# A graph attention kernel whose first layer recomputes each tile's own rows on the chip instead of loading them from its table

## The chip, the cores and the metric

The kernel runs on one core of a Trainium2 chip. The metric is the device time of one execution in microseconds (us). TensorE does the matrix products, VectorE and ScalarE the element-wise work, GpSimd issues the gathers, and SyncE issues the plain loads and stores. In the rows they are PE, DVE, ACT, POOL and SP; SPq is SyncE's queue of transfers.

## The reference

`x` is 8192 x 128, `adj` is 8192 x 8192 of int32 with about nine ones in a row, the diagonal among them. Two layers follow one another:

```
h = relu(layernorm(x))
# layer 0
wh = h @ W;  s1 = wh @ a[:128];  s2 = wh @ a[128:]
e = leaky_relu(s1[i] + s2[j], 0.2) where adj[i, j] > 0, else -9e15
x = x + elu(softmax(e) @ wh)
h = relu(layernorm(x))
# layer 1
q = h @ Wq.T + bq;  k = h @ Wk.T + bk;  v = h @ Wv.T + bv
x = x + elu(softmax(q @ k.T / sqrt(128) where adj > 0) @ v)
```

## The kernel before

A row of `adj` is nearly empty, so the kernel never forms the 8192 x 8192 scores. It reads `adj` once, finds each row's neighbours, and gathers their rows from a table in HBM. The nodes are cut into 64 tiles of 128 rows, one row to a partition.

**Setup.** Every row of `x` is measured on VectorE (`rstd`, `shift`), normalised on ScalarE, turned and projected on TensorE, two tiles a step. The result, 132 words a node (`wh`, then `s2`, `s1` and a one), goes to `table0` in HBM. `s1` also stays on the chip in `self_s1`.

**Survey**, which makes layer 0. It is a pipeline written out by hand: an iteration `t` does a different step for several tiles, and every engine runs its own list in order. For tile `t + 1` ScalarE turns four quarters of 1 MB of `adj` (`read_quarter`, L1166) to a mask, and TensorE packs the mask in 16 matmuls (`pack`, L1368). VectorE extracts tile `t`'s neighbours (`extract`, L698) and lists them. For tile `t - 3` (`PICK`) it marks (L790) and picks the indices (L820), TensorE deals (L1429), and GpSimd issues nine gathers of 128 rows into `Gt[:, t % 4, 1:]` (L571). For tile `u = t - 6` (`LATE`) VectorE makes the scores (`score0`, L836), TensorE scatters them (L1401), and VectorE takes the maxima (`maxima`, L845 to L849). For tile `w = t - 7` (`DONE`) VectorE weighs (L859), adds seven rows (`add_slot`, L869 and L866), each between two extractions, TensorE sums the rest (`sum_up`, L1415), and VectorE adds both (`total`, L875) and finishes the tile. Slot 0 of `Gt` holds the tile's own row, since every node is its own neighbour: SyncE loads it from `table0` (`load_self`, L460) tile `t - 4` in iteration `t`, 66 KB a tile, in the same queue as the loads of `adj`.

SyncE issues the next quarter of `adj` when ScalarE has read the one whose place it takes (L447). Two tiles, eight quarters, can be under way. Each pair of tiles has its list decoded in the odd iteration, which makes that one longer on VectorE; the odd iteration starts with `split` (L783), which waits for a matmul at the end of TensorE's even iteration (L1453).

**Layer 1** starts when all of the survey is done. Its rows are gathered from `table1` (L601), and its own rows are loaded there too (L521).

Of the kernel before, what the change touches and what calls it, by code (L numbers as in the profile page):

```python
# [5 lines left out]
P = 128  # L6
# [6 lines left out]
ALU = mybir.AluOpType  # L13
# [17 lines left out]
OWN = 1 + REGULAR  # L31
# [10 lines left out]
def two_layer_graph_attention(nc, x, adj, W, a, Wq, bq, Wk, bk, Wv, bv, out):  # L42
# [22 lines left out]
    with ExitStack() as ctx:  # L65
# [44 lines left out]
        neg_diag = place([T])  # L110
        self_s1 = place([T, 2])
        sum_all = place([T, QUARTERS])
        count_all = place([T])
# [13 lines left out]
        owned_list = place([GROUP, CHUNKS, DEALT])  # L127
        owned = owned_list[:, :, :, 0:P]
        early = top[0]
        Gt = place([GROUP, ROWS, WIDTH])  # L130
        weighted = place([CHUNKS, P])
        acc_sb = place([2, WIDTH])
        l10 = place([2, ROWS])
# [3 lines left out]
        gap = place([2, CHUNKS])  # L137
        p10 = place([2, ROWS])
        rinv = place([2, 1])
# [18 lines left out]
        sd = place([T])  # L158
        rstd = place([T])
        shift = place([T])  # L160
        h_rows = place([2, 2, D])
# [87 lines left out]
        ends_ps = bank(7)[:, 0:2]  # L249
        bad_ps = bank(7)[0:1, 104:105]  # L250

# [59 lines left out]
        rows_in = [sem(f"rows_in{k}") for k in range(GROUP)]  # L311
        self_in = [sem(f"self_in{k}") for k in range(GROUP)]
        e_done = sem("e_done")
        score_done = sem("score_done")
# [86 lines left out]

        PICK, LATE, DONE = 3, 6, 7
        PAIRS = T // 2
        UNITS = T // 2
# [37 lines left out]
        def _(sp):  # L442
# [15 lines left out]

            def load_self(v, k):
                sp.dma_start(Gt[:, k, 0, :], table0[bass.ds(v * P + 1, P), :]).then_inc(self_in[k], 16)  # L460

            def load_group(g):
                for b in range(GROUP):
                    s = g * GROUP + b
                    if live(s, -2):
                        for q in range(QUARTERS):

                            sp.wait_ge(mask_done, QUARTERS * s + q + 1)
                            load_adj(s + 2, b % 2, q)
                    if isinstance(s, int) and s == 5:  # L470
                        sp.wait_ge(zeros_in, 32)
                        for k in range(4):
                            sp.wait_ge(table0_in[k], 16 * UNITS // 4)
                        load_self(0, 0)
                    if not isinstance(s, int) or 5 <= s < T + 4:

                        at_least(sp, summed, s - 7)
                        load_self(s - 4, b)
                    if b == 2 and (not isinstance(g, int) or 0 <= g - 3 < G):
                        sp.wait_ge(stage_done, (g - 2) * GROUP)  # L480
                        sp.dma_start(table1[1:N + 1, :].rearrange("(t p) d -> p t d", p=P)
                                     [:, bass.ds((g - 3) * GROUP, GROUP), :], stage[:, :, :]).then_inc(table1_in, 16)
# [124 lines left out]
        def _(dve):  # L607
# [225 lines left out]
            def score0(u, k, r, n):  # L833
                dve.wait_ge(rows_in[r], 16 * (ROWS - 1) * n)
                dve.wait_ge(self_in[r], 16 * n)
                nc.vector.tensor_scalar(e10[:, 0:OWN], Gt[:, r, 0:OWN, D], self_s1[:, u, 1:2], None, ALU.add).then_inc(e_done, 1)  # L836
                nc.vector.tensor_tensor(e10[:, OWN:ROWS], Gt[:, r, OWN:ROWS, D], owned_list[:, r, :, DEALT - 1], ALU.add)\
                  .then_inc(e_done, 1)
                dve.wait_ge(e_done, 2 * u + 2)
                nc.vector.scalar_tensor_tensor(out=l10[:, k, :], in0=e10[:, :], scalar=ALPHA, in1=e10[:, :],  # L840
                                               op0=ALU.mult, op1=ALU.max).then_inc(score_done, 1)
                spread_scores(u, k, r)
# [19 lines left out]
            def add_slot(tt, k, r, c, width):  # L862

                if c:
                    dve.wait_ge(chained, OWN * tt + c)
                    nc.vector.scalar_tensor_tensor(out=acc_sb[:, k, 0:width], in0=Gt[:, r, c, 0:width], scalar=p10[:, k, c:c + 1],  # L866
                                                   in1=acc_sb[:, k, 0:width], op0=ALU.mult, op1=ALU.add).then_inc(chained, 1)
                else:
                    nc.vector.tensor_scalar(acc_sb[:, k, 0:width], Gt[:, r, 0, 0:width], p10[:, k, 0:1], None, ALU.mult)\  # L869
                      .then_inc(chained, 1)  # L870

            def total(tt, k, width):
# [55 lines left out]
            def survey(g):  # L928
                for b in range(GROUP):
# [14 lines left out]
                    for n in range(PARTS):  # L944
                        if n < OWN and live(t, DONE):
                            add_slot(w, w % 2, w % GROUP, n, D + 3)
                        if live(t, 0):
                            extract(t, b, n)
                    if live(t, LATE):
                        maxima(u, u % 2)  # L950
# [135 lines left out]
            with dve.Else():  # L1086
# [20 lines left out]
                def score1(u, b, k, n):  # L1107
                    dve.wait_ge(rows_in[b], 16 * (ROWS - 1) * n)
                    dve.wait_ge(self_in[b], 16 * n)
                    dve.wait_ge(own_done, u + 1)  # L1110
# [12 lines left out]
                def attend(g):  # L1123
                    for b in range(GROUP):
# [13 lines left out]
                        if live(t, 2):  # L1138
                            dve.wait_ge(e_done, 2 * T + t - 1)
                            maxima(T + t - 2, k)  # L1140
# [16 lines left out]
        def _(act):  # L1157
# [44 lines left out]
            def survey(g):  # L1202
                for b in range(GROUP):
# [24 lines left out]
                    if live(t, DONE):  # L1228
                        post(w, w % 2, acc_sb[:, w % 2, 0:D])
                    quarter(3)  # L1230
                    if t < 3:
# [114 lines left out]
        def _(pe):  # L1346
# [72 lines left out]
            def survey(g):  # L1419
                for b in range(GROUP):  # L1420
# [11 lines left out]
                    if live(t, DONE):  # L1432
                        at_least(pe, summed, w - 1)
                        sum_up(w, w % 2, w % GROUP, D + 3)
                    if live(t, -1):

                        at_least(pe, top_done, t)
                        pack(t + 1, (b + 1) % 2, range(0, 8))
# [5 lines left out]
                    if t < 3:  # L1444
                        for i in range(12 * t, min(12 * t + 12, UNITS)):
                            turn_rows(i)
                            if i:
                                project_rows(i - 1)
                        if t == 2:
                            project_rows(UNITS - 1)  # L1450
                    if b % 2 == 0 and live(t, 2):
                        pe.wait_ge(count_done, 4 * (t // 2))
                        nc.tensor.matmul(ends_ps, upto[:, :], over16[:, :], start=True, stop=True).then_inc(ends_done, 1)  # L1453
                    if t == T + 4:
                        pe.wait_ge(bad_done, 9)
                        nc.tensor.matmul(bank(7)[:, 104:105], ones[:, 0:P], bad_row[:, :], start=True, stop=True)\
                          .then_inc(bad_summed, 1)
# [58 lines left out]
            with pe.Else():  # L1516

                def attend(g):
                    for b in range(GROUP):
# [17 lines left out]
                        if live(t, 0):  # L1537
                            pe.wait_ge(self_in[b], 16 * (G + g + 1))
                            at_least(pe, u_kept, t)
# [36 lines left out]
```

## Time and profile before

| | us |
|---|---|
| median of 3 runs | 1697.23 (1695.82 to 1697.98) |
| the profiled execution | 1699.37 |
| its span | 1697.6 |
| VectorE, GpSimd, TensorE busy in the span | 1201.7, 1137.3, 1189.3 |

The page cuts the span in 40 slices of 42.4 us. The DMA engines are busy for nine tenths in all of the first twenty, and two tenths or so from there on: the survey ends near 860 us, and layer 1 begins near 950 us. A busy time is not a bound by itself. What ends last in each stage is told by the chain and by the waits.

### The profile page before, as it was taken

The numbers are of one execution on the slowest core, as the hardware profiler recorded it, in microseconds if no ns is written. First come the engines' busy times: TensorE is split into PE (matmuls) and PEld (weight loads), VectorE is DVE, ScalarE is ACT, GpSimd is POOL, SyncE is SP. The second block draws the span as 40 slices with busy tenths as digits, with TensorE's granted clock in tenths as the row PEclk, the third lists the DMA queues.
The fourth block names the chain that finished last, engine by engine and source line by source line (L and its number), as shares of the span: only waits on it lengthen the run. The fifth ranks groups of instructions, "written<-read, shape, count | busy, mean of one in ns | idle before, by whom it ended". The sixth has DMA issues, their size and how long they took to land.

```text
span 1697.6 us, 23065 instructions
## 1 busy us (share of the span) xinstructions
PE 1189.3 (70%) x5362; PEld 930.2 (55%) x5362; DVE 1201.7 (71%) x6497; ACT 904.9 (53%) x1827; POOL 1137.3 (67%) x1206
## 2 busy tenths in 40 slices
PE   2667777777777777777765467776777677676665
PEld 1344545545545554544455466766666566666664
DVE  3567988888888888888887366656655665566655
ACT  2769877877878778887852222333233323332322
POOL 1227777766766666666666477777777777777773
PEclk9778777777777777777765555556665666666755
DMA  9869999999999999999942122222222222222221
GB/s 292 345 225 391 397 398 399 400 401 396 390 386 394 365 371 390 382 394 371 386 125 61 51 59 57 65 64 66 64 66 64 66 64 64 66 64 64 66 66 39
DMA packets 122263, 372.41 MB, mean 219 GB/s; under 512 B 34577, under 2 KB 67858, under 8 KB 89362
## 3 DMA queue, kind: packets, MB, share of 16 engines
q1 hardware_dynamic: 75458, 289.83, 44.3%
q0 software_dynamic: 38464, 81.08, 17.1%
q10 hardware_dynamic: 8208, 0.03, 0.3%
q8 instruction: 46, 0.75, 0.2%
q14 instruction: 87, 0.71, 0.1%
HBM read 358.12 MB, written 12.72 MB: 218 GB/s over the span
## 4 chain that ended last, share of the span: by engine, by line
DMA 40%; POOL 33%; issue 13%; ACT 5%; DVE 4%; PE 3%; SPq 2%; POOLq 0%; ACTq 0%; DVEq 0%
DMA arena<-in_adj_dram 37%; POOL arena L601 32%; ACT arena L1166 4%; DMA table<-arena 1%; POOL arena L571 1%; SPq L444 1%; DMA arena<-table 1%; DVE arena L658 1%; SPq L447 1%; PE psum L1368 0%; DVE arena L866 0%; PE psum L1429 0%; DMA arena<-table,arena 0%; PE psum L1393 0%; PE psum L1415 0%
## 5 line engine op out<-in xcount | busy, mean ns | idle before, releaser
L571 POOL DMA_INDIRECT arena<-table,arena x576 | 558.7, 970 | 252.5 <-issue 164.6
L601 POOL DMA_INDIRECT arena<-table,arena x576 | 550.3, 955 | 184.0 <-issue 174.9
L1166 ACT ACTIVATE arena<-arena 128x2048 bf16<-128x2048 int32 x256 | 487.9, 1906 | 163.3 <-DMA arena<-in_adj_dram 160.7
L1368 PE MATMUL psum<-arena 128*128 128x512 bf16 x1024 | 301.6, 437 | 71.7 <-ACT arena L1166 71.3
L866 DVE SCALAR_TENSOR_TENSOR arena<-arena 128x131 f32<-128x131 f32 (+1 forms) x768 | 267.3, 348 | 15.2
L1415 PE MATMUL psum<-arena 128*128 128x131 f32 (+1 forms) x768 | 200.7, 433 | 104.1 <-ACT arena L1303 102.4
L1401 PE MATMUL psum<-arena 128*128 128x18 f32 x768 | 144.6, 321 | 143.7 <-DVE arena L830 143.2
L1415 PEld LDWEIGHTS psum<-arena 128*128 128x128 f32 x768 | 179.9, 330 | 107.7 <-issue 107.7
L1368 PEld LDWEIGHTS psum<-arena 128*128 128x128 bf16 x1024 | 111.3, 118 | 221.2 <-ACT arena L1166 90.7
L1401 PEld LDWEIGHTS psum<-arena 128*128 128x128 f32 x768 | 138.5, 265 | 161.9 <-DVE arena L830 161.8
L1112 DVE CUSTOM_DVE_ANT_0 arena<-arena,psum 128x129 f32<-128x129 f32 x192 | 45.2, 286 | 226.4 <-DMA arena<-table,arena 226.4
L1408 PE MATMUL psum<-arena 128*128 128x1 f32 x768 | 137.1, 294 | 94.0 <-DVE arena L849 93.9
L1408 PEld LDWEIGHTS psum<-arena 128*128 128x128 f32 x768 | 138.1, 257 | 117.2 <-DVE arena L849 108.4
L1196 ACT ACTIVATE arena<-arena 128x7 f32<-128x7 f32 x128 | 37.9, 296 | 231.8 <-DVE arena L849 231.8
L1324 ACT ACTIVATE arena<-psum 128x384 f32<-128x384 f32 x64 | 31.5, 492 | 236.4 <-PE psum L1535 236.4
L1429 PE MATMUL psum<-arena 128*128 128x155 f32 x384 | 117.7, 476 | 27.3 <-DVE arena L790 26.9
L1534 PE MATMUL psum<-arena 128*128 128x128 f32 x384 | 119.0, 412 | 1.0 <-DVE arena L1104 1.0
L1535 PE MATMUL psum<-arena 128*128 128x129 f32 x384 | 116.7, 404 | 0.0
L1429 PEld LDWEIGHTS psum<-arena 128*128 128x128 f32 x384 | 94.8, 317 | 31.9 <-DVE arena L790 31.4
L1534 PEld LDWEIGHTS psum<-arena 128*128 128x128 f32 x384 | 103.7, 329 | 1.5 <-issue 1.5
L698 DVE MAX8 arena<-psum 128x8 f32<-128x64 f32 x512 | 104.4, 221 | 0.0
L1118 DVE CUSTOM_DVE_ANT_0 arena<-arena 128x129 f32<-128x129 f32 x448 | 101.1, 290 | 0.0
(197 smaller groups left out, 1951.7 us busy)
## 6 DMA issues: line engine op xcount, KB each, us to landing
arena<-in_adj_dram SPq DMA_DIRECT2D x256, 1024.0 KB, 22.4
arena<-table,arena POOLq DMA_INDIRECT x1152
table<-arena POOLq DMA_DIRECT2D x32, 132.0 KB, 4.5
arena<-table SPq DMA_DIRECT2D x64, 66.0 KB, 17.5
table<-arena SPq DMA_DIRECT2D x16, 256.0 KB
arena<-table SPq DMA_DIRECT2D x64, 64.0 KB, 1.9
out_dram<-arena SPq DMA_DIRECT2D x16, 256.0 KB, 2.4
arena<-in_x_dram SPq DMA_DIRECT2D x4, 0.5 KB, 12.1
```

Source lines behind the costliest of these rows:

```text
L571: pool.indirect_dma_start(Gt[:, v % GROUP, c + 1, :], None, table0, bass.IndirectOffsetOnAxis(idx_now[:, v % GROUP, c:c + 1], 0))\
L601: pool.indirect_dma_start(Gt[:, t % GROUP, c + 1, 0:D], None, table1, bass.IndirectOffsetOnAxis(idx_now[:, t % GROUP, c:c + 1], 0))\
L698: ins = nc.vector.max(words[:, b // 2, b % 2, 8 * n:8 * n + 8], V[b % 2][:, PLACE * n:PLACE * (n + 1)])
L866: nc.vector.scalar_tensor_tensor(out=acc_sb[:, k, 0:width], in0=Gt[:, r, c, 0:width], scalar=p10[:, k, c:c + 1], in1=acc_sb[:, k, 0:width] ...
L1166: nc.scalar.activation(mask[:, k, q * QUARTER:(q + 1) * QUARTER], adj_sb[:, k, q, :], ACT.Relu, accum_out=sum_all[:, bass.ds(tile, 1), q:q ...
L1368: nc.tensor.matmul(V[k], shifted[:, s, :], mask[:, k, s * 512:(s + 1) * 512], start=(s == 0), stop=False)
L1401: last = nc.tensor.matmul(by_slot_ps[k], owned[:, r, c, :], slot_e[:, k, c, :], start=(c == 0), stop=(c == CHUNKS - 1))
L1408: last = nc.tensor.matmul(max_ps[k][:, c:c + 1], mine[:, r, c * P:(c + 1) * P], neg_max[:, k, :], start=True, stop=True)
L1415: last = nc.tensor.matmul(acc_ps[k][:, 0:width], weighted[:, c, :], Gt[:, r, OWN + c, 0:width], start=(c == 0), stop=(c == CHUNKS - 1))
L1429: last = nc.tensor.matmul(deal_ps[v % 2][:, c, :], mine[:, v % GROUP, c * P:(c + 1) * P], dealt[:, v % GROUP, :], start=True, stop=True)
L1534: nc.tensor.matmul(own_ps[m][:, c, :], mine_c, ident[:, :], start=True, stop=True)
L1535: last = nc.tensor.matmul(uq_ps[m][:, c, :], mine_c, u_row[:, j, P:], start=True, stop=True)
```

## The change

In layer 0 the tile's own row is no longer loaded. ScalarE normalises the tile's 128 rows again from `X` in iteration `t = o + 4` (`NORM`), into slot 0 of `Gt`. In iteration `o + 5` (`TURN`) TensorE transposes them to PSUM, VectorE copies them to `self_hT`, and TensorE multiplies by `ww`, which gives `wh`, `s2` and `s1` of the tile in PSUM (`self_ps`, two places in bank 7). `score0` reads the own row's `s2` there in an instruction of its own, and `add_self` takes the place of the first `add_slot`. SyncE's 64 loads of the first table are gone. `rstd` and `shift` move to a place that is kept, and the accumulator is laid so that its last column is the own row's probability, which the load's column of ones gave before. The second layer still loads its own rows; only the counts of its waits differ. A matmul for the check at the end of the survey moves to bank 2.

```diff
-        acc_sb = place([2, WIDTH])
+        sums_p = place([2, D + 2 + ROWS])
+        acc_sb = sums_p[:, :, 0:D + 3]
+        p10 = sums_p[:, :, D + 2:]
...
+        self_ps = [bank(7)[:, 4 + (D + 2) * k:4 + (D + 2) * (k + 1)] for k in range(2)]
+        self_turned_ps = bank(7)[:, 384:384 + P]
...
+        NORM, TURN = 4, 5
...
-            def load_self(v, k):
-                sp.dma_start(Gt[:, k, 0, :], table0[bass.ds(v * P + 1, P), :]).then_inc(self_in[k], 16)
...
-                    if isinstance(s, int) and s == 5:
-                        sp.wait_ge(zeros_in, 32)
-                        for k in range(4):
-                            sp.wait_ge(table0_in[k], 16 * UNITS // 4)
-                        load_self(0, 0)
-                    if not isinstance(s, int) or 5 <= s < T + 4:
-
-                        at_least(sp, summed, s - 7)
-                        load_self(s - 4, b)
...
             def score0(u, k, r, n):
                 dve.wait_ge(rows_in[r], 16 * (ROWS - 1) * n)
-                dve.wait_ge(self_in[r], 16 * n)
-                nc.vector.tensor_scalar(e10[:, 0:OWN], Gt[:, r, 0:OWN, D], self_s1[:, u, 1:2], None, ALU.add).then_inc(e_done, 1)
+                dve.wait_ge(self_done, u + 1)
+                nc.vector.tensor_scalar(e10[:, 0:1], self_ps[k][:, D:D + 1], self_s1[:, u, 1:2], None, ALU.add).then_inc(e_done, 1)
+                nc.vector.tensor_scalar(e10[:, 1:OWN], Gt[:, r, 1:OWN, D], self_s1[:, u, 1:2], None, ALU.add).then_inc(e_done, 1)
...
+            def add_self(tt, k):
+                nc.vector.tensor_scalar(acc_sb[:, k, 0:D + 2], self_ps[k], p10[:, k, 0:1], None, ALU.mult).then_inc(chained, 1)
+
+            def keep_self_turned(o):
+                dve.wait_ge(self_turned, o + 1)
+                nc.vector.tensor_copy(self_hT[:, :], self_turned_ps).then_inc(self_hT_done, 1)
...
                     for n in range(PARTS):
-                        if n < OWN and live(t, DONE):
+                        if n == 0 and live(t, DONE):
+                            add_self(w, w % 2)
+                        elif n < OWN and live(t, DONE):
                             add_slot(w, w % 2, w % GROUP, n, D + 3)
                         if live(t, 0):
                             extract(t, b, n)
+                    if live(t, TURN):
+                        keep_self_turned(t - TURN)
                     if live(t, LATE):
                         maxima(u, u % 2)
...
                     if live(t, DONE):
                         post(w, w % 2, acc_sb[:, w % 2, 0:D])
+                    if live(t, NORM):
+                        o = t - NORM
+                        at_least(act, self_turned, o - GROUP + 1)
+                        nc.scalar.activation(Gt[:, o % GROUP, 0, 0:D], X[:, o, :], ACT.Relu, bias=shift[:, o:o + 1],
+                                             scale=rstd[:, o:o + 1]).then_inc(self_h_done, 1)
                     quarter(3)
...
                         sum_up(w, w % 2, w % GROUP, D + 3)
+                    if live(t, TURN):
+                        o = t - TURN
+                        pe.wait_ge(self_h_done, o + 1)
+                        at_least(pe, chained, OWN * (o - 2) + 1)
+                        nc.tensor.transpose(self_turned_ps, Gt[:, o % GROUP, 0, 0:D], ident[:, :]).then_inc(self_turned, 1)
...
+                    if live(t, TURN):
+                        o = t - TURN
+                        pe.wait_ge(self_hT_done, o + 1)
+                        nc.tensor.matmul(self_ps[o % 2], self_hT[:, :], ww[:, :], start=True, stop=True).then_inc(self_done, 1)
                     if b % 2 == 0 and live(t, 2):
                         pe.wait_ge(count_done, 4 * (t // 2))
                         nc.tensor.matmul(ends_ps, upto[:, :], over16[:, :], start=True, stop=True).then_inc(ends_done, 1)
```

TensorE before, one even iteration of the survey: scatter, deal, sum, eight packs, the maxima's spread (L1408), eight packs, the end of the pack, and the matmul that `split` waits for.

```order
L1401 MATMUL psum<-arena 128x18 x3
L1429 MATMUL psum<-arena 128x155 x3
L1415 MATMUL psum<-arena 128x131 x3
L1368 MATMUL psum<-arena 128x512 x8
L1408 MATMUL psum<-arena 128x1 x3
L1368 MATMUL psum<-arena 128x512 x8
L1374 MATMUL psum<-arena 128x128
L1375 MATMUL psum<-arena 128x512
L1453 MATMUL psum<-arena 128x2
```

TensorE now, the same iteration (L1415, L1443, L1429, L1382 and L1422 are the lines of scatter, deal, sum, pack and spread in the changed file).

```order
L1415 MATMUL psum<-arena 128x18 x3
L1443 MATMUL psum<-arena 128x155 x3
L1429 MATMUL psum<-arena 128x131 x3
L1453 MATMUL psum<-arena 128x128
L1382 MATMUL psum<-arena 128x512 x8
L1422 MATMUL psum<-arena 128x1 x3
L1382 MATMUL psum<-arena 128x512 x8
L1388 MATMUL psum<-arena 128x128
L1389 MATMUL psum<-arena 128x512
L1473 MATMUL psum<-arena 128x130
L1476 MATMUL psum<-arena 128x2
```

The transpose (L1453) stands behind the sum and ahead of the first pack, the projection (L1473) behind the last.

VectorE before, from the last extraction of an iteration to the sum of tile `w`.

```order
L866 SCALAR_TENSOR_TENSOR arena<-arena 128x131
L698 MAX arena<-psum 128x8 x2
L845 TENSOR_TENSOR arena<-arena 128x7
L847 TENSOR_TENSOR arena<-psum,arena 128x18
L849 TENSOR_REDUCE arena<-arena 128x1
L875 TENSOR_TENSOR arena<-psum,arena 128x131
```

VectorE now, the same place (L875 is the new copy, L843 to L847 are the maxima and L880 is `total` in the changed file).

```order
L864 SCALAR_TENSOR_TENSOR arena<-arena 128x131
L695 MAX arena<-psum 128x8 x2
L875 COPY arena<-psum 128x128
L843 TENSOR_TENSOR arena<-arena 128x7
L845 TENSOR_TENSOR arena<-psum,arena 128x18
L847 TENSOR_REDUCE arena<-arena 128x1
L880 TENSOR_TENSOR arena<-psum,arena 128x131
```

The copy, which waits for TensorE's transpose of the same iteration, stands ahead of the maxima and of `total`.

## Rows read from the trace of the kernel before

**Rows 1.** the chain that ended last, by engine (page, part 4; shares of the span).

```profile
DMA 40%; POOL 33%; issue 13%; ACT 5%; DVE 4%; PE 3%; SPq 2%; POOLq 0%; ACTq 0%; DVEq 0%
```

**Rows 2.** busy time of the engines in both stages; us, then busy us (count) each.

```profile
148.00:857.00 709.00, 538.36 (x2368) 360.20 (x2368) 607.13 (x3209) 564.23 (x851) 491.35 (x507) 0.77 1.01 389
950.00:1672.00 722.00, 514.38 (x2387) 469.99 (x2387) 432.47 (x2499) 214.04 (x743) 547.33 (x573) 0.61 0.25 64
```

**Rows 3.** DMA queues and issues in the survey, 148 to 857 us.

```profile
GB/s 400 396 398 396 399 396 399 397 400 403 397 401 402 398 390 398 403 376 385 404 372 393 398 333 387 399 351 380 399 373 396 374 374 402 384 346 400 379 387 382
...
q1 hardware_dynamic: 46574, 240.58, 86.2%
...
arena<-in_adj_dram SPq DMA_DIRECT2D x219, 1024.0 KB, 22.8
...
arena<-table SPq DMA_DIRECT2D x56, 66.0 KB, 17.6
```

**Rows 4.** DMA queue q1 in the second layer, 1100 to 1500 us.

```profile
q1 hardware_dynamic: 9792, 4.66, 4.0%
```

**Rows 5.** waits of VectorE, 148 to 857 us: total us, times, longest.

```profile
DVE arena L859 <- ACT arena L1200: 29.2, 36, 1.8
DVE arena L783 <- PE psum L1453: 24.1, 21, 2.1
DVE arena L875 <- PE psum L1415: 5.6, 14, 0.6
```

**Rows 6.** waits of ScalarE in the same stretch.

```profile
ACT arena L1166 <- DMA arena<-in_adj_dram: 133.5, 145, 2.8
```

**Rows 7.** six tiles in order of time: start us, us, engine, line.

```profile
172.25 0.14 DVE L845 TENSOR_TENSOR arena<-arena 128x7 f32<-128x7 f32 x1
...
173.05 3.15 PE L1368 MATMUL psum<-arena 128*128 128x512 bf16 x8
...
182.56 1.89 PE L1368 MATMUL psum<-arena 128*128 128x512 bf16 x8
...
183.70 0.15 DVE L845 TENSOR_TENSOR arena<-arena 128x7 f32<-128x7 f32 x1
...
195.45 0.14 DVE L845 TENSOR_TENSOR arena<-arena 128x7 f32<-128x7 f32 x1
...
196.16 1.89 PE L1368 MATMUL psum<-arena 128*128 128x512 bf16 x8
...
207.48 0.14 DVE L845 TENSOR_TENSOR arena<-arena 128x7 f32<-128x7 f32 x1
...
208.08 2.70 PE L1368 MATMUL psum<-arena 128*128 128x512 bf16 x8
...
220.75 0.15 DVE L845 TENSOR_TENSOR arena<-arena 128x7 f32<-128x7 f32 x1
...
221.54 2.79 PE L1368 MATMUL psum<-arena 128*128 128x512 bf16 x8
...
231.24 3.06 PE L1368 MATMUL psum<-arena 128*128 128x512 bf16 x8
...
232.00 0.14 DVE L845 TENSOR_TENSOR arena<-arena 128x7 f32<-128x7 f32 x1
```

**Rows 8.** costliest groups, 50 to 130 us: count | busy us, mean ns.

```profile
L1393 PE MATMUL psum<-arena 128*128 128x130 f32 x128 | 26.1, 337 | 10.3 <-DVE arena L685 10.3
...
L1174 ACT ACTIVATE arena<-arena 128x128 f32<-128x128 f32 x64 | 26.1, 482 | 9.9 <-PE psum L1385 9.9
...
L1385 PE MATMUL psum<-arena 128*128 128x128 f32 x64 | 14.1, 309 | 0.0
...
L685 DVE COPY arena<-psum 128x256 f32<-128x256 f32 x32 | 13.3, 417 | 14.8 <-PE psum L1385 14.8
```

**Rows 9.** VectorE at the first tile's scores.

```profile
147.03 0.23 DVE L836 TENSOR_SCALAR arena<-arena 128x7 f32<-128x7 f32 x1 [2.00 <-DMA arena<-table]
```

**Rows 10.** the same view as rows 8, 80 to 860 us.

```profile
L869 DVE TENSOR_SCALAR arena<-arena 128x131 f32<-128x131 f32 x55 | 15.5, 282 | 0.0
```

More of the change, by code:

```diff
@@ L111, in two_layer_graph_attention @@
         self_s1 = place([T, 2])
+        rstd = place([T])
+        shift = place([T])
         sum_all = place([T, QUARTERS])
@@ L128, in two_layer_graph_attention @@
         owned = owned_list[:, :, :, 0:P]
+        self_hT = place([P])
         early = top[0]
@@ L137, in two_layer_graph_attention @@
         gap = place([2, CHUNKS])
-        p10 = place([2, ROWS])
         rinv = place([2, 1])
@@ L158, in two_layer_graph_attention @@
         sd = place([T])
-        rstd = place([T])
-        shift = place([T])
         h_rows = place([2, 2, D])
@@ L249, in two_layer_graph_attention @@
         ends_ps = bank(7)[:, 0:2]
-        bad_ps = bank(7)[0:1, 104:105]
+        bad_ps = bank(2)[0:1, 480:481]
+        self_ps = [bank(7)[:, 4 + (D + 2) * k:4 + (D + 2) * (k + 1)] for k in range(2)]
+        self_turned_ps = bank(7)[:, 384:384 + P]
         own_ps = [bank(k)[:, 0:CHUNKS * P].rearrange("p (c q) -> p c q", c=CHUNKS) for k in range(2)]
@@ L312, in two_layer_graph_attention @@
         self_in = [sem(f"self_in{k}") for k in range(GROUP)]
+        self_h_done = sem("self_h_done")
+        self_turned = sem("self_turned")
+        self_hT_done = sem("self_hT_done")
+        self_done = sem("self_done")
         e_done = sem("e_done")
@@ L834, in score0 @@
                 dve.wait_ge(rows_in[r], 16 * (ROWS - 1) * n)
-                dve.wait_ge(self_in[r], 16 * n)
-                nc.vector.tensor_scalar(e10[:, 0:OWN], Gt[:, r, 0:OWN, D], self_s1[:, u, 1:2], None, ALU.add).then_inc(e_done, 1)
+                dve.wait_ge(self_done, u + 1)
+                nc.vector.tensor_scalar(e10[:, 0:1], self_ps[k][:, D:D + 1], self_s1[:, u, 1:2], None, ALU.add).then_inc(e_done, 1)
+                nc.vector.tensor_scalar(e10[:, 1:OWN], Gt[:, r, 1:OWN, D], self_s1[:, u, 1:2], None, ALU.add).then_inc(e_done, 1)
                 nc.vector.tensor_tensor(e10[:, OWN:ROWS], Gt[:, r, OWN:ROWS, D], owned_list[:, r, :, DEALT - 1], ALU.add)\
                   .then_inc(e_done, 1)
-                dve.wait_ge(e_done, 2 * u + 2)
+                dve.wait_ge(e_done, 3 * u + 3)
                 nc.vector.scalar_tensor_tensor(out=l10[:, k, :], in0=e10[:, :], scalar=ALPHA, in1=e10[:, :],
@@ L1108, in score1 @@
                     dve.wait_ge(rows_in[b], 16 * (ROWS - 1) * n)
-                    dve.wait_ge(self_in[b], 16 * n)
+                    dve.wait_ge(self_in[b], 16 * (n - G))
                     dve.wait_ge(own_done, u + 1)
@@ L1138, in attend @@
                         if live(t, 2):
-                            dve.wait_ge(e_done, 2 * T + t - 1)
+                            dve.wait_ge(e_done, 3 * T + t - 1)
                             maxima(T + t - 2, k)
@@ L1455, in survey @@
                         pe.wait_ge(bad_done, 9)
-                        nc.tensor.matmul(bank(7)[:, 104:105], ones[:, 0:P], bad_row[:, :], start=True, stop=True)\
+                        pe.wait_ge(owned_done, T)
+                        nc.tensor.matmul(bank(2)[:, 480:481], ones[:, 0:P], bad_row[:, :], start=True, stop=True)\
                           .then_inc(bad_summed, 1)
@@ L1537, in attend @@
                         if live(t, 0):
-                            pe.wait_ge(self_in[b], 16 * (G + g + 1))
+                            pe.wait_ge(self_in[b], 16 * (g + 1))
                             at_least(pe, u_kept, t)
```

## Prediction

> **What bounds the kernel now.** I read the chain of waits first: the DMA engines hold 40% of it and GpSimd 33% [rows 1]. The stages part the two. In the survey, from 148 us (the first tile's scores) to 857 us (the last quarter of `adj`), the DMA engines are busy all the time (share 1.01, 389 GB/s); in layer 1 they are a quarter busy, and GpSimd, issuing gathers, works for 547 of 722 us with its own issue gaps between [rows 2]. The change touches nothing in layer 1 but counts of waits, so I leave it at its time. Everything is decided in the survey.
>
> How long is a tile there? Queue q1 moved 240.58 MB [rows 3]. Off that go 56 own-row loads of 67.6 KB (3.79 MB) and the stores of `table1`, 12 of 262 KB or 3.15 MB by the code; 233.6 MB of `adj` at 4.194 MB a tile are 55.7 tiles. 709 us over 55.7 is 12.73 us a tile.
>
> Then I ask how near the next engine is. ScalarE waits for `adj` 133.5 us in that stretch [rows 6], 2.4 us a tile: it has room. VectorE is busy 607 of 709 us [rows 2], and its waits are small: 29.2 us for ScalarE's L1200, 24.1 us for the matmul behind the even pack, 5.6 us for the sum [rows 5], 58.9 us together. ScalarE reaches L1200 behind a quarter of `adj`, and the pack waits for the mask, so the first two are mostly DMA time seen from VectorE. Without any wait VectorE needs (709 - 59) / 55.7 = 11.67 us a tile. It stands 1.06 us a tile behind the DMA, and that is all the room that the new work has.
>
> **What the change removes.** (a) The loads: 3.79 of the 275.6 MB that went at 389 GB/s over 709 us [rows 2], 9.7 us. By packets instead: layer 1's q1 used 4.0% of 16 engines for 400 us on 9792 packets of some 500 bytes, 26 ns each [rows 4]; 56 x 128 of them on 16 engines are 11.7 us. I take 10.5 us, 0.19 a tile: the DMA's tile falls to 12.54 us. (b) The first tile's scores waited 2.00 us for the own-row load after the gathers [rows 9]; that wait goes, 2 us at most, and the gathers may be just behind it. (c) SyncE's issue of the loads: it waits for ScalarE anyway, so nothing.
>
> **What it adds.** ScalarE: one 128x128 activation a tile, 0.48 us by the row for that form [rows 8]. It stands ahead of quarter 3, but ScalarE has 2.4 us a tile of waiting: nothing, and 0.4 us a tile (22 us) if that cover were gone. TensorE: a projection of 0.34 us and a transpose of 0.31 us [rows 8], ahead of which the pack waits for masks anyway; nothing by itself.
>
> VectorE: the score of the own row, one instruction of one element. It overlaps its neighbours; I take 0.10 us, between 0 and the 0.23 us of the seven-element one [rows 9]. `add_self` replaces an instruction of 0.28 us [rows 10] by one that is an element shorter, same price, with 0 to 0.07 us more. The copy of 128 columns from PSUM: the 256-column one took 0.417 us [rows 8]; half is 0.21, which I take, the whole is the upper end.
>
> The new wait is the term that matters. The copy waits for the transpose, which TensorE issues behind `sum_up` of the same iteration, where the first pack starts now; the maxima and `total` are queued behind it on VectorE, then everything to the end of the iteration, and TensorE's spread and ScalarE's probabilities wait for the maxima. Before, VectorE went on to L845 whatever TensorE did. In six tiles one after another L845 starts at 172.25, 183.70, 195.45, 207.48, 220.75 and 232.00, and the first pack at 173.05, 182.56, 196.16, 208.08, 221.54 and 231.24 [rows 7]. The transpose would be issued at that start and end 0.31 us later, so the stall is (pack - L845 + 0.31) where positive: 1.11, 0, 1.02, 0.91, 1.10 and 0. The zeros are the iterations in which TensorE ran its sum fast. With copy and score (0.31) the mean added is 4.14 / 6 + 0.31 = 1.00 us a tile. These tiles have hardly a wait for ScalarE in them, as VectorE would run where it is the bound, so they are the right ones to take. `total` waited for the sum before, which the 5.6 us above already took out. Bounds: 0.31 if TensorE is always early, 1.11 + 0.52 = 1.6 if it is always late and the copy dear.
>
> **Page and row.** The Trainium skill (VectorE: DVE Perf Modes, Why PSUM operands drop a tier) says that an fp32 operand in PSUM holds VectorE to one element a cycle, where a single source in SBUF may go at two. For `add_self` that speaks against the change; I estimate from the page's 0.96 GHz 130 / 0.96 GHz / 2 = 0.07 us a tile, and by it the sum would be 4 us longer. No row here shows the two sources side by side; the 131-column one from SBUF took 0.28 us [rows 10], so the difference stays outside the sum.
>
> **The sum.** VectorE's tile becomes 11.67 + 1.00 = 12.67 us, against 12.54 of the DMA. The survey goes at the larger one: 12.67 - 12.73 = -0.06 us, over 55.7 tiles -3.3 us; the first wait gives -2. Further, the even iteration now ends on TensorE 0.34 us later, which `split` may see: between 0 and 28 x 0.34 = 9.5 us, I take 2, since that wait is mostly for the mask. The drain behind 857 us is gather-bound and keeps its length. Together about -3 us: the profiled execution would go from 1699.4 to 1696.4. It stands 2.1 us above the median of the runs, so I predict 1694 us for the median.
>
> **Rivals.**
> 1. The DMA stays the bound and the whole saving shows. VectorE's added work is below 0.87 us a tile if TensorE stays fast in the odd iterations and in some even ones, because its gaps get shorter. For it: the two zeros above. Against it: four of six are late. Then -10.5 - 2 = -12.5, 1685 us.
> 2. Slower: the serial chain VectorE to TensorE to VectorE. The mark releases the deal, then sum, transpose, copy, maxima, all inside one iteration, and each new iteration starts on the end of TensorE's last (`self_done`, which every `score0` waits for). If the waits for ScalarE and for `split` stay partly, because those are in the chain too, they do not pay for the stall. It decides from 1.06 us a tile on. With half of the 53.3 us of the first two waits staying, the sum is -3 + 27 = +24; with a quarter +10. I take +15 as its centre: 1712 us. For it: 12.54 beside 12.67 leaves no slack for jitter between the engines. Against it: up to eight quarters of `adj` can be stored ahead.
> 3. The change frees bytes but the survey does not go faster, as the rate of the DMA varies (333 to 404 GB/s in slices [rows 3]) for reasons outside the queue: only the first 2 us, 1695 us.
>
> **Chances.** Forecast (the two bounds meet) 0.48, its own range 1688 to 1702; rival 1 0.20; rival 2 0.27; rival 3 0.05. For the whole range I take 1684, which holds most of rival 1, to 1713, half of rival 2. A change under 0.2%, 3.4 us, can't be told from none here. Faster, below 1693.8: 0.23 of the forecast's 0.48, and 0.20 of rival 1, 0.43. Slower, above 1700.6: 0.05 of the forecast and 0.25 of rival 2, 0.30. The same: 0.27.
>
> **What would show it.** The saving: 64 fewer loads, and q1 3.8 MB lighter in the survey. The bound: ScalarE's waits for `adj` fall far below 133.5 us, the DMA share below 1.0, and VectorE's waits for ScalarE and at `split` nearly go. The stall: a new VectorE wait for the transpose of 0.5 to 0.9 us a tile, 30 to 50 us in all; under 20 us is rival 1, and with it a share of 1.01 as before. For rival 2 that wait stands beside 20 us or more of the old ones, and the last quarter of `adj` lands after 857 us. I am wrong altogether if layer 1 (950 to 1672 us) changes its length, or if the drain between does.

## The result, and the profile after

| | before, us | after, us |
|---|---|---|
| median of 20 runs | 1695.80 (1694.05 to 1699.98) | 1700.66 (1698.25 to 1703.53) |
| the profiled execution | 1699.37 | 1698.98 |
| its span | 1697.6 | 1697.2 |

The changed kernel is slower, by 4.9 us between the medians; the ratio of the paired runs is 1.0024 (95% interval 1.0017 to 1.0030), which is 4.1 us. The two profiled executions differ by 0.4 us only, the changed kernel's being the shorter. That of before was one of its slower ones, 3.6 us above its median, and that of after lies 1.7 us below its own. The traces tell where time is spent, then, but the sum is read from the runs.

The chain of the changed kernel by engine (the page, part 4), against [rows 1]:

```profile
POOL 33%; DVE 27%; PE 20%; issue 13%; ACT 4%; DMA 2%; SPq 1%; POOLq 0%; ACTq 0%; DVEq 0%
```

GpSimd's third is layer 1, as before. The DMA engines' 40% have become 2%, and VectorE and TensorE, which held 7% together, hold 47%. So the survey is bound by another thing. The engines in the two stages, the windows and columns of [rows 2]:

```profile
148.00:857.00 709.00, 551.27 (x2486) 381.08 (x2529) 621.13 (x3314) 585.93 (x911) 485.59 (x505) 0.77 1.00 382
950.00:1672.00 722.00, 503.26 (x2387) 460.20 (x2387) 433.50 (x2500) 214.87 (x744) 546.13 (x574) 0.63 0.25 64
```

Layer 1 has the same load on every engine. From its first gather to its last it takes 724.5 us before and 723.4 after; the twelve traces of this document have 723.1 to 725.2, so 1.1 us is no more than they differ by anyway. In the survey VectorE works 621 us instead of 607. The DMA share is still 1.00, although nobody waits for it, as the next rows show. The queue in that stretch, against [rows 3]:

```profile
q1 hardware_dynamic: 38338, 236.13, 84.5%
...
arena<-in_adj_dram SPq DMA_DIRECT2D x218, 1024.0 KB, 12.2
```

8236 packets are gone, most of them the own rows. A quarter of `adj` now lands 12.2 us after its issue, where it took 22.8. At 382 and 389 GB/s I estimate from this that some 4 quarters are on their way, where there were some 8: the queue is no longer full. The waits of VectorE and ScalarE, 148 to 857 us, against [rows 5, 6]:

```profile
DVE arena L875 <- PE psum L1453: 43.7, 50, 1.4
DVE arena L780 <- PE psum L1476: 6.3, 14, 0.9
```

```profile
ACT arena L1205 <- DVE arena L847: 69.5, 54, 1.7
ACT arena L1209 <- DVE arena L851: 30.5, 27, 1.8
ACT arena L1234 <- PE psum L1443: 9.1, 13, 0.8
ACT arena L1187 <- DVE arena L783: 8.1, 15, 0.7
```

VectorE waits 43.7 us for the transpose (L1453), in 50 of the 56 tiles. In this stretch ScalarE's 133.5 us of waits for `adj` are gone altogether, and it waits for VectorE's maxima instead. One even iteration shows how (start, duration, engine, line; L1429 is the sum, L875 the copy, L843 the maxima):

```profile
274.58 1.52 PE L1429 MATMUL psum<-arena 128*128 128x131 f32 x6
...
274.89 0.35 DVE L695 MAX8 arena<-psum 128x8 f32<-128x64 f32 x2
...
275.89 0.40 PE L1453 MATMUL psum<-arena 128*128 128x128 f32 x1
...
276.33 0.29 DVE L875 COPY arena<-psum 128x128 f32<-128x128 f32 x1 [1.08 <-PE psum L1453]
276.53 0.16 DVE L843 TENSOR_TENSOR arena<-arena 128x7 f32<-128x7 f32 x1
```

VectorE ends its extractions at 275.24 and stands still until the transpose is through at 276.29. The odd iteration ahead of it has the same wait, a third as long:

```profile
261.50 0.42 PE L1453 MATMUL psum<-arena 128*128 128x128 f32 x1
...
261.96 0.29 DVE L875 COPY arena<-psum 128x128 f32<-128x128 f32 x1 [0.36 <-PE psum L1453]
```

Where the time goes is read from one instruction that every iteration has, the deal. Its rows for the 1st, 5th, 11th, 57th and 61st tile that have a scatter ahead of it, first of before, then of after:

```profile
148.86 1.90 PE L1429 MATMUL psum<-arena 128*128 128x155 f32 x6
...
193.24 1.90 PE L1429 MATMUL psum<-arena 128*128 128x155 f32 x6
...
269.02 1.92 PE L1429 MATMUL psum<-arena 128*128 128x155 f32 x6 [0.66 <-DVE arena L790]
...
862.09 1.92 PE L1429 MATMUL psum<-arena 128*128 128x155 f32 x6 [1.12 <-DVE arena L790]
...
905.49 1.90 PE L1429 MATMUL psum<-arena 128*128 128x155 f32 x6
```

```profile
146.32 1.80 PE L1443 MATMUL psum<-arena 128*128 128x155 f32 x6
...
194.80 1.92 PE L1443 MATMUL psum<-arena 128*128 128x155 f32 x6
...
272.89 1.90 PE L1443 MATMUL psum<-arena 128*128 128x155 f32 x6
...
861.35 1.90 PE L1443 MATMUL psum<-arena 128*128 128x155 f32 x6
...
907.80 1.90 PE L1443 MATMUL psum<-arena 128*128 128x155 f32 x6
```

| us a tile | before | after |
|---|---|---|
| first 4 | 11.10 | 12.12 |
| next 6 | 12.63 | 13.02 |
| next 46 | 12.89 | 12.79 |
| last 4 | 10.85 | 11.61 |

The survey before had two bounds in turn. What ScalarE waited for `adj`, from 148 to 200 us and then from 200 to 269 us:

```profile
ACT arena L1166 <- DMA arena<-in_adj_dram: 0.5, 1, 0.5
...
ACT arena L1166 <- DMA arena<-in_adj_dram: 13.1, 15, 2.8
```

In the first four tiles ScalarE hardly waited for `adj`, so the DMA did not bound them, and the new work on VectorE and its wait cost 4.1 us there. From 200 us on the DMA was the bound. The next six tiles lose another 2.3 us, and the 46 behind them win 4.6 us.

The last four deals come 3.1 us further apart in all, but what counts there is when the gathers end and layer 1 can start. From 856 to 930 us GpSimd waits for VectorE's indices as follows, first before, then after; below it stands layer 1's first gather of each:

```profile
POOL arena L571 <- DVE arena L820: 5.1, 3, 2.8
...
POOL arena L568 <- DVE arena L817: 6.8, 6, 2.2
```

```profile
950.16 0.95 POOL L601 DMA_INDIRECT arena<-table,arena  x1 [8.74 <-DVE arena L1090]
...
951.25 0.95 POOL L598 DMA_INDIRECT arena<-table,arena  x1 [8.73 <-DVE arena L1099]
```

From the 57th deal to layer 1 it is 88.1 us before and 89.9 us after: the drain is 1.8 us longer, about as much as GpSimd waits longer (1.7 us).

The first deal is 2.5 us earlier, and the first score waits for no load. How much of it that load was worth can't be told: the eight traces without the wait for it have their first deal anywhere from 146.3 to 149.8 us, the four with it from 147.6 to 150.5 us.

### The profile page after: what moved, and what is told of

Same layout as the page of the kernel before. It is cut to its first block, busy times and chain, and to the rows that moved or that the text cites. A ratio compares the mean times of both kernels' runs of the same rounds, so it can differ in the third digit from the quotient of the medians.

```text
span 1697.2 us, 23466 instructions
## 1 busy us (share of the span) xinstructions
PE 1195.3 (70%) x5503; PEld 944.0 (56%) x5554; DVE 1220.4 (72%) x6625; ACT 928.7 (55%) x1891; POOL 1131.2 (67%) x1206
## 4 chain that ended last, share of the span: by engine, by line
POOL 33%; DVE 27%; PE 20%; issue 13%; ACT 4%; DMA 2%; SPq 1%; POOLq 0%; ACTq 0%; DVEq 0%
POOL arena L598 32%; PE psum L1443 6%; PE psum L1429 4%; PE psum L1415 4%; ACT arena L1175 3%; PE psum L1382 3%; DVE arena L754 2%; DVE arena L757 2%; DMA table<-arena 1%; DVE arena L880 1%; DVE arena L864 1%; DVE arena L875 1%; DVE arena L892 1%; DVE arena L889 1%; DVE arena L827 1%
## 5 line engine op out<-in xcount | busy, mean ns | idle before, releaser
L1382 PE MATMUL psum<-arena 128*128 128x512 bf16 x973 | 283.7, 428 | 51.5 <-ACT arena L1175 46.8
L1429 PE MATMUL psum<-arena 128*128 128x131 f32 (+1 forms) x768 | 200.6, 433 | 103.8 <-ACT arena L1317 102.1
L1415 PE MATMUL psum<-arena 128*128 128x18 f32 x768 | 145.1, 322 | 166.1 <-DVE arena L827 165.7
L1415 PEld LDWEIGHTS psum<-arena 128*128 128x128 f32 x768 | 138.4, 265 | 185.0 <-DVE arena L827 184.7
L1429 PEld LDWEIGHTS psum<-arena 128*128 128x128 f32 x768 | 179.1, 329 | 107.5 <-issue 107.5
L1382 PEld LDWEIGHTS psum<-arena 128*128 128x128 bf16 x1024 | 110.0, 116 | 189.0 <-issue 67.4
L1422 PE MATMUL psum<-arena 128*128 128x1 f32 x768 | 134.7, 291 | 108.0 <-DVE arena L847 108.0
L1422 PEld LDWEIGHTS psum<-arena 128*128 128x128 f32 x768 | 134.6, 251 | 132.8 <-DVE arena L847 124.1
L1443 PE MATMUL psum<-arena 128*128 128x155 f32 x384 | 114.4, 466 | 4.6 <-DVE arena L787 4.6
## 6 DMA issues: line engine op xcount, KB each, us to landing
arena<-in_adj_dram SPq DMA_DIRECT2D x256, 1024.0 KB, 12.2
arena<-in_x_dram SPq DMA_DIRECT2D x4, 0.5 KB, 12.2
```

The lines of the kernel that those rows point to most:

```text
L1382: nc.tensor.matmul(V[k], shifted[:, s, :], mask[:, k, s * 512:(s + 1) * 512], start=(s == 0), stop=False)
L1415: last = nc.tensor.matmul(by_slot_ps[k], owned[:, r, c, :], slot_e[:, k, c, :], start=(c == 0), stop=(c == CHUNKS - 1))
L1422: last = nc.tensor.matmul(max_ps[k][:, c:c + 1], mine[:, r, c * P:(c + 1) * P], neg_max[:, k, :], start=True, stop=True)
L1429: last = nc.tensor.matmul(acc_ps[k][:, 0:width], weighted[:, c, :], Gt[:, r, OWN + c, 0:width], start=(c == 0), stop=(c == CHUNKS - 1))
L1443: last = nc.tensor.matmul(deal_ps[v % 2][:, c, :], mine[:, v % GROUP, c * P:(c + 1) * P], dealt[:, v % GROUP, :], start=True, stop=True)
```

## The experiments

Each was timed (4 to 11 executions) beside the kernel before on the same chip. The first four ran together, with the kernel before at 1695.76 us; the next four had it at 1695.83 us, and the last two, on another chip, at 1698.69 us. Between groups the ratios are the fairer measure.

**The copy behind `total`.** VectorE's list only:

```diff
                     for n in range(PARTS):
...
-                    if live(t, TURN):
-                        keep_self_turned(t - TURN)
                     if live(t, LATE):
                         maxima(u, u % 2)
                     if live(t, DONE):
                         total(w, w % 2, D + 3)
+                    if live(t, TURN):
+                        keep_self_turned(t - TURN)
```

> The changed kernel with VectorE's copy of the transposed rows moved from ahead of the maxima to behind total. Theory A (the survey is bound by VectorE's work plus its stall for the transpose, 44.7 us in 51 waits): the stall goes, 0.8 us a tile, VectorE needs about 12.0 us a tile, the DMA bounds again at 12.54 us, and the kernel ends at 1684 to 1688 us, some 10 us below the kernel before; ScalarE's waits for adj come back to 80 us or more. Rival B (the order VectorE to TensorE to VectorE is not the matter, VectorE's, ScalarE's and TensorE's added work is; the wait only shows where the slack lies): the wait turns up elsewhere, at total, at split or before the scatter, and the time stays within 3 us of 1701. Rival C (the rate of adj is what it is, whatever else the queue holds): 1694 to 1697.

Measured 1684.22 us (1683.27 to 1686.36), ratio to before 0.9932 (0.9920 to 0.9945). The waits of VectorE from 148 to 857 us:

```profile
DVE arena L780 <- PE psum L1476: 14.6, 19, 2.0
DVE arena L880 <- PE psum L1429: 13.3, 32, 0.5
DVE arena L857 <- ACT arena L1209: 2.4, 4, 1.1
DVE arena L875 <- PE psum L1453: 1.6, 1, 1.6
```

The 43.7 us for the transpose have become 1.6. Some waiting turns up at `total` instead (L880, 13.3 us, where the kernel before had 5.6), but it does not set the time, as ScalarE waits for `adj` again (146 to 846 us):

```profile
ACT arena L1175 <- DMA arena<-in_adj_dram: 65.9, 98, 2.1
```

That is less than theory A had said (80 us). That the DMA is the bound again is shown further down, where loads put back cost 10.4 us in this version. Two lines moved are worth 16.4 us, the difference of the medians (15.6 us by the ratios): theory A, against B and C.

**The transpose early.** TensorE's list, and another bank for the transpose's result:

```diff
-        self_turned_ps = bank(7)[:, 384:384 + P]
+        self_turned_ps = [bank(4 + (k + 1) % 2)[:, 256:256 + P] for k in range(2)]
...
+                    if live(t, TURN):
+                        o = t - TURN
+                        pe.wait_ge(self_h_done, o + 1)
+                        at_least(pe, summed, t - DONE)
+                        nc.tensor.transpose(self_turned_ps[o % 2], Gt[:, o % GROUP, 0, 0:D], ident[:, :]).then_inc(self_turned, 1)
                     if live(t, LATE):
                         scatter(u, u % 2, u % GROUP)
...
-                    if live(t, TURN):
-                        o = t - TURN
-                        pe.wait_ge(self_h_done, o + 1)
-                        at_least(pe, chained, OWN * (o - 2) + 1)
-                        nc.tensor.transpose(self_turned_ps, Gt[:, o % GROUP, 0, 0:D], ident[:, :]).then_inc(self_turned, 1)
...
                         pe.wait_ge(self_hT_done, o + 1)
+                        at_least(pe, chained, OWN * (o - 2) + 1)
```

> The changed kernel with the transpose moved on TensorE from behind the sum to the start of the iteration, where TensorE waits for VectorE's scores anyway (2.4 us a tile), into the other accumulator bank; VectorE's order is as in the changed kernel. Theory A: the copy finds its data ready, no stall, 1684 to 1688 us as with the copy moved. Rival B: within 3 us of 1701. A version between A and B would be one in which TensorE's own list matters: the sum then ends 0.4 us earlier, which no theory prices at more than 1 us.

Measured 1684.27 us (1679.93 to 1686.85), ratio 0.9926 (0.9913 to 0.9939). The same time from the other end of the wait, with VectorE's order untouched. The bank is not what counts, since the version above keeps it and ends at the same time. VectorE's waits in 146 to 846 us hold none for the copy (the three longest), and ScalarE waits 77.7 us for `adj`:

```profile
DVE arena L780 <- PE psum L1477: 20.9, 19, 2.4
DVE arena L880 <- PE psum L1429: 5.1, 18, 0.3
DVE arena L833 <- PE psum L1474: 3.7, 3, 2.2
```

**Four loads in place of 64, in the kernel before.** It leaves 60 of the own-row loads out, so that later tiles take old rows for their own. The counts of two waits of layer 1 are changed to fit.

```diff
-                    if not isinstance(s, int) or 5 <= s < T + 4:
+                    if isinstance(s, int) and 5 <= s < 8:
 
                         at_least(sp, summed, s - 7)
                         load_self(s - 4, b)
...
-                dve.wait_ge(self_in[r], 16 * n)
+                dve.wait_ge(self_in[r], 16)
```

> The kernel before, in which the own-row loads are made for the first tiles only, one for each of the four slots; the 60 others are left out, so later tiles use old rows in slot 0, with the same work on every engine. It prices what leaving the loads out gives where nothing is added. By bytes 9.7 us, by packets 11.7 us, and up to 2 us at the first score if that load is the wait there (it is kept here, so this part should not show): 1684 to 1687 us. Rival C (the rate of adj does not depend on the other packets): 1694 to 1696 us.

Measured 1684.37 us (1682.59 to 1688.58), ratio 0.9935 (0.9923 to 0.9948). The loads are worth 11.4 us, near the price by packets (11.7) that part (a) of the prediction had beside that by bytes. This is the time that both repaired versions reach (1684.22 and 1684.27 us), so the new work, placed well, costs nothing that shows.

**The transpose twice.**

```diff
+                        nc.tensor.transpose(self_turned_ps, Gt[:, o % GROUP, 0, 0:D], ident[:, :])
                         nc.tensor.transpose(self_turned_ps, Gt[:, o % GROUP, 0, 0:D], ident[:, :]).then_inc(self_turned, 1)
```

> The changed kernel with the transpose issued twice in a row, the second one signalling. Theory A: the stall grows by one more transpose, 0.22 to 0.42 us a tile, and the survey with it: 57 x 0.22 to 0.42 = 13 to 24 us, so 1714 to 1725 us, and the waits for the transpose grow from 45 us to about 60 to 68. Rival B: VectorE's total work is unchanged and the time moves by less than 3 us.

Measured 1711.32 us (1709.7 to 1714.45), ratio 1.0090 (1.0077 to 1.0104), 10.7 us above the changed kernel's median, and 52.4 us of waits for the copy:

```profile
DVE arena L875 <- PE psum L1454: 52.4, 50, 2.0
DVE arena L780 <- PE psum L1477: 4.1, 14, 0.8
```

The direction is theory A's and excludes B. The size is below its range, of the time (1714 to 1725 us) and of the waits: from 140 to 870 us, where the changed kernel waits 44.7 us, they are 56.4 us, not 60 to 68. 0.19 us a tile is about the 0.22 us that stood between the starts of the transpose and the first pack (275.89 and 276.11), not the 0.40 us of one's length.

**The loads put back beside the new work.** Both versions load 80 words a row to a place that nobody reads:

```diff
+            def load_self(v, k):
+                sp.dma_start(spare[:, k, :], table0[bass.ds(v * P + 1, P), 0:80]).then_inc(self_in[k], 16)
...
+                        at_least(sp, summed, s - 7)
+                        load_self(s - 4, b)
...
+                dve.wait_ge(self_in[r], 16 * n)
                 dve.wait_ge(self_done, u + 1)
```

In the changed kernel:

> The changed kernel with the loads of the own rows put back beside the new work, into a spare place of 80 words a row (320 bytes, the same 64 loads and 8192 rows as before), read by nobody; the first score waits for them again. Theory A (VectorE and its stall bound the changed kernel, with the DMA below its limit): the loads fit into the DMA's room of 12.80 - 12.54 us a tile or nearly so, 1700 to 1705 us. Rival C (the queue is still a bound in the changed kernel, so that the loads' removal was worth its 10 us there too): 1708 to 1712 us.

Measured 1702.42 us (1699.96 to 1704.2), ratio 1.0041 (1.0027 to 1.0055): 1.8 us above the changed kernel (2.9 us by the ratios). With the copy behind `total`:

> The same loads put back into the version with the copy behind total. There the DMA is the bound, so they cost their price again, 128 x 60 rows at the per-row price of layer 1's queue (26 ns, 12 us) or by bytes 6 us: 1690 to 1697 us, against 1684 without. This is the kernel before with all of the new work added and no stall: near 1696 would say that the new work without the stall is free.

Measured 1694.67 us (1691.89 to 1696.21), ratio 0.9992 (0.9983 to 1.0001): 10.4 us above the version without. The same 64 loads cost 10 us where the DMA is the bound and 2 to 3 us in the changed kernel. And the second of these is the kernel before with all of the new work on top (its loads are shorter, 320 bytes a row in place of 528), at the time of the kernel before.

**ScalarE's normalisation behind quarter 3.**

```diff
-                    if live(t, NORM):
-                        o = t - NORM
...
                     quarter(3)
+                    if live(t, NORM):
+                        o = t - NORM
```

> The changed kernel with ScalarE's second normalisation moved from ahead of quarter 3 to behind it. The mask of quarter 3 comes 0.39 us earlier, TensorE's pack and the matmul that split waits for with it. Theory A in its narrow form (stall and VectorE's work, 6.3 us of waits at split): at most those 6.3 us, 1695 to 1699 us. Rival B' (ScalarE's list is part of the loop: maxima, probabilities, normalisation, quarter 3, pack, next iteration): up to 0.39 x 57 = 22 us, down to the DMA's 1684. If nothing but VectorE counts: 1700 to 1701.

Measured 1698.01 us (1695.07 to 1700.48), ratio 1.0017 (1.0008 to 1.0026): 2.6 us below the changed kernel. By the ratios it is 1.2 us, and their intervals overlap, so the change of the waits is clear and that of the time is not. VectorE's waits, 146 to 858 us:

```profile
DVE arena L875 <- PE psum L1453: 45.1, 52, 1.3
DVE arena L780 <- PE psum L1476: 2.0, 3, 1.2
```

The wait at `split` falls from 6.3 to 2.0 us, and the one for the transpose does not fall. What the place in ScalarE's list costs is at most these 4 us of waits, not the up to 22 us of B'.

**A second copy on VectorE**, to a spare place, in the changed kernel and in the version with the copy behind `total`:

```diff
+                nc.vector.tensor_copy(spare[:, :], self_turned_ps)
                 nc.vector.tensor_copy(self_hT[:, :], self_turned_ps).then_inc(self_hT_done, 1)
```

> The changed kernel with a second copy of the same 128 columns by VectorE, ahead of the one that signals. If VectorE's list bounds the changed kernel, all of it shows: 0.21 us a tile by the start-to-start in the trace, 57 x 0.21 = 12 us, 1711 to 1714 us. If slack is left in the even or in the odd iterations (split's waits, 0.11 us a tile), 6 to 9 us: 1706 to 1710.

Measured 1714.78 us (1711.23 to 1716.4), ratio 1.0113 (1.0097 to 1.0129), 14.1 us above the changed kernel, at the upper end of the 1711 to 1714 us written down: 0.2 us of VectorE a tile shows in full there.

> The version with the copy behind total, with the second copy too. If the DMA bounds it and VectorE has the room that 12.54 against about 12.0 us a tile says, most of the 0.21 us a tile is hidden: 1684 to 1689 us, where the same copy cost the changed kernel 14 us. If VectorE is as near as it was there: 1695 to 1698.

Measured 1690.84 us (1685.88 to 1692.7), ratio 0.9960 (0.9946 to 0.9974). The ratio is 0.0028 above that of the version with one copy, some 5 us: about two thirds of it is hidden. The kernel before was at 1698.69 us here; at the 1695.8 us of the other groups the ratio gives 1689 us, the upper end of what I had written for room on VectorE (1684 to 1689). Where the 5 us go isn't shown, since the profiled execution was the fastest of the six, 1685.88 us.

**Early transpose and late normalisation together**, the edits of both.

> The version with the early transpose and, on top, ScalarE's normalisation behind quarter 3. If the DMA bounds both versions at its floor, nothing moves: 1682 to 1686 us. If the split waits of 20.9 us that are left there cost something, some of 0.39 us a tile comes back: 1678 to 1681.

Measured 1685.13 us (1684.01 to 1685.28), ratio 0.9923 (0.9909 to 0.9936), against 0.9926 for the early transpose alone. With the wait for the transpose out of the way, the place of the normalisation is worth nothing that shows, although 20.3 us of waits at `split` are left.

## Why the prediction was wrong

The forecast was 1694 us, a little faster by its centre; it became slower, 1700.66 us against 1695.80.

- **The bound of before, and the saving.** Right. 56 loads at 0.19 us a tile were to give 10.5 us; leaving out 60 gives 11.4.
- **The mechanism.** Right. The new wait of VectorE for the transpose makes VectorE the bound: 43.7 us in 50 waits against the 30 to 50 us written down. Moving either side of it gives 16.4 us.
- **The step that failed is the size of VectorE's waits in its tile.** The sum had 0.69 us a tile for the transpose and 0.04 for `split`, which with 11.67 + 0.31 of work makes 12.71 us. Measured are 43.7 + 6.3 us over 55.5 tiles, 0.79 + 0.11 us, and the 56 tiles between the first and the 57th deal are 12.77 us each where the kernel before had 12.74. VectorE's added work, counted as the prediction counts it, was priced too high and not too low: (709 - 50) / 55.5 = 11.87 us without any wait, 0.20 above 11.67, where the sum had 0.31 for the copy and the score. The two errors partly cancel, and 0.06 us over 56 tiles, some 3 us, remain.
- **The six tiles of [rows 7] were a poor sample.** The same arithmetic (pack - L845 + 0.31, where positive) over all 56 tiles of before gives a mean of 0.61 us and a zero in three tiles, not in two of six; and of the two zeros only one had a fast sum (0.83 us; the other 1.38). The transpose was priced at 0.31 us from the setup stage, and in the survey it takes 0.405. With that length the 56 tiles give 0.70. So the 0.69 of the sum was near this by luck, and the last 0.09 up to the measured 0.79 is unexplained. The groups from 80 to 860 us (count | busy, mean ns | idle before):

```profile
L1453 PE MATMUL psum<-arena 128*128 128x128 f32 x57 | 23.1, 405 | 0.0
L871 DVE TENSOR_SCALAR arena<-psum,arena 128x130 f32<-128x130 f32 x55 | 18.8, 342 | 0.0
L875 DVE COPY arena<-psum 128x128 f32<-128x128 f32 x57 | 16.5, 290 | 44.9 <-PE psum L1453 44.9
```

- **`split`** waited 6.3 us, 0.11 a tile, where I had 2 us. The experiment with ScalarE's normalisation behind quarter 3 shows that two thirds of it come from ScalarE's 0.48 us ahead of quarter 3. I had called these hidden because ScalarE waited for `adj`, and that cover went with the DMA bound itself.
- **`add_self`** was left outside the sum at 0.07 us a tile, an estimate by the Trainium skill (VectorE: DVE Perf Modes, Why PSUM operands drop a tier). The trace agrees in the length of the instruction: 0.342 us against the 0.282 of [rows 10], 0.06 us more. What it cost the kernel was not tested. The starts of the instructions give more added work (0.06 for `add_self`, 0.21 for the copy, 0.13 for the score) than the 0.20 us above; why the two ways of counting differ is open.
- **The drain** was said to keep its length. It is 1.8 us longer.
- **The start** was to give 2 us. The first deal is 2.5 us earlier, within what the traces differ by.
- **From the profiled execution to the median.** The sum gave 1696.4 us for the profiled execution, and 1698.98 were measured, 2.6 us more. The other 4 us of the 6.7 lie in the step to the median: I took 2.1 us off, because the profiled execution of before lay above its median, but that of the changed kernel lies 1.7 us below its own. Part of the miss of the median is thus chance in which executions were profiled.
- **Rivals.** Rival 1's floor, 1685, is what the repaired versions reach. Rival 2 had the sign, and the place in the chain VectorE to TensorE to VectorE; but its condition, that half or a quarter of the old waits stay, did not come true: of 53.3 us 6.3 are left, all at `split`. I had given 0.30 to any slower outcome. Rival 3 is excluded by the kernel before without the loads.
- **What would show it.** ScalarE's waits for `adj` and VectorE's old waits did as written. The DMA share was to fall below 1.0 and did not.

The bounds of the term were known: 0.31 to 1.6 us a tile around a room of 1.06. A forecast of 1.00 beside a room of 1.06 could not tell the sign from six tiles.

What stays open is why the profiled execution of before ran its 46 tiles at 12.89 us when the version without loads had 12.65 in its own: the difference, 0.24, is above the 0.19 to 0.20 of the loads. One trace of each does not tell this from the spread of executions.

## What to carry to other kernels

When recomputing replaces a load, look at where the recomputed value's own chain is cut into the engines' lists. A producer behind three other steps of one engine's iteration and a consumer in the middle of the other's, in the same iteration, make a wait. Here it was enough to put the consumer behind four short instructions (some 0.7 us later, an estimate from the rows above), or the producer ahead of the scatter (4.1 us earlier by the same rows: 275.89 against 271.82): either was worth 16 us.

When the room on the second engine is as thin as the new work, price that work in the stage where it runs, take the wait from all tiles of the trace and not from six, and add what was hidden behind the bound that goes away. A bound averaged over a stage can be two bounds in turn: here the DMA did not bound the first four tiles.

## What the runs showed of the hardware

- The DMA engines' busy share stayed at 1.00 in the changed kernel's survey, in which ScalarE had no wait for `adj` and the time to landing had halved (22.8 to 12.2 us). The waits and the time to landing told the bound here, the share did not.
- Loads of 128 rows of 528 bytes cost 11.4 us for 60, 0.19 us each; of 320 bytes 10.4 us for 64. From the first price I estimate 12.2 us for the 64 if it goes by rows and 7.4 us if by bytes; the measured 10.4 us lies between, nearer to the rows.
- The fp32 transpose of 128 x 128 took 309 ns on average in the setup stage (granted clock 0.81 from 50 to 130 us) and 405 ns in the survey (0.77). The median was 273 ns in the setup stage and 421 ns in the survey, and both lengths occur in both.
